# Linear attention with top-1 expert routing: scores by halves of 32 keys, masks of 512 columns, and denominators, logits and ranks in weight sets of 128 columns

## The chip, the cores and the metric

The kernel runs on one core of a Trainium2 chip. The metric is the device time of one execution in microseconds; lower is better. Before the change three runs gave 335.36, 336.8 and 338.79 us, median 336.8 us.

## The reference

One transformer block over x of shape (2, 2048, 128), all in fp32: layer norm and modulation, causal linear attention with 16 heads of 8, a projection, a second norm and modulation, a gate that gives each token one of 8 experts, and that expert's two layers.

```python
q, k, v = jnp.split(h @ w_attn, 3, axis=-1)     # each split into 16 heads of 8
q = elu(q) + 1.0;  k = elu(k) + 1.0
# for every token t, running over all earlier tokens and itself:
#   S += k_t (x) v_t ;  z += k_t ;  y_t = (q_t S) / (q_t . z + 1e-6)
x = x + ga * (y @ w_proj)
h = layernorm(x) * (1 + cb) + sb
logits = h @ Wg + bg;  expert = argmax(logits)
x = x + gb * (gelu(h @ W1[expert]) @ W2[expert])
```

## The kernel before

The 4096 tokens are 32 tiles of 128. A group is four tiles, two consecutive ones (s = 0, 1) of each of the two sequences (b = 0, 1); there are eight groups. Attention inside a tile goes by chunks of L = 64 tokens: what earlier chunks give comes through a running state (`core_across`, L1192 updates it, L1200 multiplies q with it), what the chunk itself gives comes from scores of its 64 keys against its 64 queries, masked so that no query sees a later key.

A unit u = 2s + half is one chunk of both sequences. Per tile, `core_scores` (L1176) makes the scores of four "quads" q of four heads each. `k_q` holds the keys with all rows but the quad's zero; `q_m` holds the queries four times, each time with all heads but one of each quad zero. One matmul has 64 keys of a chunk as weights and 2 x 64 query columns as moving data and writes 64 rows by 128 columns; its two halves (`half`, a pair of heads each) go to rows 0 to 63 and 64 to 127 of a PSUM bank. Two chunks (n) fill 256 columns. Quads alternate between two banks, S0 and S1. On VectorE `core_probs` (L750) multiplies each quad's 256 columns with the mask `causal` into `probs`; `core_within` (L1211) multiplies these with `v_m`, in four column tiles of 32. The work of a tile is issued as FIRST (quads 0, 1) and LAST (quads 2, 3). TensorE waits before each quad until the quad two before it has been masked (`probs_ready`), VectorE before each mask for its scores (`score_mm`).

The step of group g also makes the next group's q, k and v (`front_x` L1123 turns normalised tiles, ScalarE's `front_ht` L486 evacuates them, `front_qkv` L1129, L1131 and, for v, L1135), turns k (`front_kt` L1144, used as k by rows of tokens in `core_across`), makes the denominators' dot products (`front_den` L1154) and turns their reciprocals (`front_inv` L1162). It projects (`core_proj` L1225, evacuated by VectorE's `core_x1` L781). And it routes the group before it: `route_turn` L1234, `route_logits` L1242, `route_rank` L1252 on TensorE; `route_modulate` (L806, L808), `z_and_argmax` and `rden_and_slots` (ending in `slot_i`, L875) on VectorE. With `slot_i` GpSimd scatters the group's rows, tile by tile, to HBM (L411). `core_proj` waits for the slots as well, since it writes the bank that logits and ranks are read from.

`front_den`, `route_logits` and `route_rank` write four column tiles of 32 tokens each, with sets of 32 weight columns; v and turned k use sets of 64.

The order is written out by hand in one function `step` for each engine; all engines run in order and meet at semaphores. After the eight groups the expert stage takes 39 tiles of 128 sorted rows through both layers (L1314, L1321, L1330).

## Time and profile before

| | |
|---|---|
| median of three runs | 336.8 us |
| the profiled execution's own time | 336.95 us |
| its span | 335.2 us |
| PE (TensorE matmul) busy | 266.8 us, 80% |
| DVE (VectorE) busy | 219.9 us, 66% |
| ACT (ScalarE) busy | 158.0 us, 47% |
| POOL (GpSimd) busy | 151.8 us, 45% |
| L1176, scores | 1024 passes, 72.3 us busy, idle 9.1 before them |
| L750, masks | 128 of 420 ns, 51.5 us busy, idle 25.9 before them |

An fp32 matmul shows as two passes, each with its own weight load (PEld), so 512 matmuls are 1024 passes. PE's busy time counts overlapping passes once, and the end of a matmul is modelled. A row of a timeline is a run of instructions of one line: its start, how long until the last one's end, and in brackets the idle time before it with what ended it.

### The profile page before, as it was taken

Reading aid. Unit: us, or ns where it says so; the run is one execution under the profiler, and the core shown is the slowest. Engines: PE = TensorE matmul, PEld = TensorE weight load, DVE = VectorE, ACT = ScalarE, POOL = GpSimd, SP = SyncE. Lnnn points to the kernel's source line nnn. Section 1 sums busy time; section 2 is a strip of 40 time slices with the busy share of each in tenths; the row PEclk is TensorE's granted clock in tenths of the full one; section 3 lists DMA queues with packets and bytes.
Section 4 is the critical chain, followed back from the end, with each engine's and each line's share of the span. In section 5 each row is a group of like instructions: output and inputs, shape, how many; then the busy total and the mean of one; then the engine's idle time right before and its main releaser. Section 6 shows DMA issues by size and latency. Waiting matters only on the chain.

```text
span 335.2 us, 13040 instructions
## 1 busy us (share of the span) xinstructions
PE 266.8 (80%) x5095; PEld 221.5 (66%) x5095; DVE 219.9 (66%) x780; ACT 158.0 (47%) x317; POOL 151.8 (45%) x173
## 2 busy tenths in 40 slices
PE   0564898988798798699699879775949689999990
PEld 0333777676476576567557657664849689999990
DVE  4985539688579478568568768768665645455540
ACT  3059595534345146146065264004525347777740
POOL 8939600352560570471453355330354734455552
PEclk9957899999799899989979999979978959999996
DMA  7990000000100200200200110111673634444410
GB/s 212 336 304 4 0 5 4 3 5 28 72 4 5 98 2 4 98 2 4 91 9 4 57 44 4 55 47 48 182 209 111 231 107 128 128 125 143 132 41 0
DMA packets 17461, 25.85 MB, mean 77 GB/s; under 512 B 2747, under 2 KB 13117, under 8 KB 17410
## 3 DMA queue, kind: packets, MB, share of 16 engines
q1 hardware_dynamic: 13616, 16.12, 16.9%
q0 software_dynamic: 3360, 8.73, 7.3%
q8 instruction: 38, 0.62, 0.8%
q10 hardware_dynamic: 434, 0.27, 0.4%
q14 instruction: 13, 0.11, 0.1%
HBM read 14.78 MB, written 10.78 MB: 76 GB/s over the span
## 4 chain that ended last, share of the span: by engine, by line
PE 52%; DVE 24%; issue 11%; another core or an unknown queue 4%; ACT 4%; DMA 1%; POOL 1%; SPq 1%; POOLq 0%; DVEq 0%; ACTq 0%
PE bank L1176 11%; PE bank L1321 11%; PE bank L1330 10%; DVE probs L750 5%; PE bank L1129 4%; DVE z_t L815 3%; PE bank L1211 2%; DVE row_buf L808 2%; PE bank L1225 2%; DVE row_buf L806 2%; PE bank L1131 2%; DVE mean L660 2%; PE bank L1162 2%; PE bank L1314 1%
## 5 line engine op out<-in xcount | busy, mean ns | idle before, releaser
L1176 PE MATMUL bank<-q_m,k_q 128*64 128x128 f32 x1024 | 72.3, 285 | 9.1 <-DVE probs L750 5.7
L1176 PEld LDWEIGHTS bank<-q_m,k_q 128*64 128x64 f32 x1024 | 56.6, 140 | 18.8 <-DVE probs L750 9.3
L750 DVE TENSOR_TENSOR probs<-bank,causal 128x256 f32<-128x256 f32 x128 | 51.5, 420 | 25.9 <-PE bank L1176 16.5
L411 POOL DMA_INDIRECT sorted_rows<-row_buf,slot_i x32 | 31.6, 988 | 65.5 <-DVE slot_i L875 57.2
L446 POOL DMA_INDIRECT out_dram<-q_m,slot_token x39 | 38.9, 997 | 38.5 <-DVE q_m L1038 25.8
L1321 PE MATMUL bank<-q_m,k_q 128*128 128x128 f32 x312 | 44.0, 287 | 7.4 <-issue 7.4
L1321 PEld LDWEIGHTS bank<-q_m,k_q 128*128 128x128 f32 x312 | 40.4, 203 | 7.9 <-issue 7.9
L1330 PE MATMUL bank<-k_q,v_m 128*128 128x128 f32 x312 | 43.0, 283 | 1.1 <-issue 1.1
L1330 PEld LDWEIGHTS bank<-k_q,v_m 128*128 128x128 f32 x312 | 39.8, 200 | 1.5 <-issue 1.3
L1211 PE MATMUL bank<-probs,v_m 128*32 128x64 f32 x1024 | 21.9, 225 | 16.7 <-DVE probs L750 16.3
L391 POOL TENSOR_TENSOR guess<-var,minus_half 128x4 f32<-128x4 f32 x8 | 8.3, 1039 | 54.2 <-DVE var L663 54.2
L1211 PEld LDWEIGHTS bank<-probs,v_m 128*32 128x32 f32 x1024 | 17.0, 111 | 20.5 <-issue 20.5
L1021 DVE COPY k_q<-w_all 128x512 f32 x39 | 16.9, 436 | 20.6 <-PE bank L1330 17.4
L423 POOL TENSOR_TENSOR k_q<-k_t,quad_rows 128x512 f32<-128x512 f32 x24 | 27.4, 1173 | 2.3 <-DVE k_t L732 2.3
L603 ACT ACTIVATE v_m<-bank 128x512 f32<-128x512 f32 x39 | 23.2, 594 | 9.8 <-PE bank L1321 7.7
L592 ACT ACTIVATE k_q<-w_all 128x512 f32 x39 | 24.4, 630 | 4.1 <-issue 3.6
L545 ACT ACTIVATE h_t<-bank 128x512 f32<-128x512 f32 x8 | 4.8, 598 | 43.4 <-PE bank L1234 43.2
L598 ACT ACTIVATE q_m<-bank 128x128 f32<-128x128 f32 x39 | 10.8, 277 | 23.7 <-PE bank L1314 11.0
L505 ACT ACTIVATE q_m<-q_t,quad_head 128x512 f32<-128x512 f32 x32 | 20.4, 710 | 0.0
L486 ACT ACTIVATE h_t<-bank,sa_col,ca_col 128x256 f32<-128x256 f32 x16 | 8.2, 560 | 25.5 <-PE bank L1123 21.7
L541 ACT ACTIVATE rden<-bank 128x512 f32<-128x512 f32 x8 | 4.8, 597 | 29.9 <-PE bank L1162 29.8
L1135 PEld LDWEIGHTS bank<-wqkv,h_t 128*64 128x64 f32 x256 | 9.0, 151 | 8.6 <-issue 8.6
(208 smaller groups left out, 493.4 us busy)
## 6 DMA issues: line engine op xcount, KB each, us to landing
v_m<-sorted_rows SPq DMA_DIRECT2D x23, 196.0 KB, 2.3
x_all<-in_L_attn_x_dram SPq DMA_DIRECT2D x16, 128.0 KB, 4.2
w_all<-in_L_ffn_W_dram SPq DMA_DIRECT2D x1, 2048.0 KB, 8.7
probs<-sorted_rows SPq DMA_DIRECT2D x10, 196.0 KB, 2.2
sorted_rows<-zeros SPq DMA_DIRECT2D x8, 196.0 KB
q_m<-sorted_rows SPq DMA_DIRECT2D x6, 196.0 KB, 2.6
out_dram<-q_m,slot_token POOLq DMA_INDIRECT x39
sorted_rows<-row_buf,slot_i POOLq DMA_INDIRECT x32
```

Of the source, the lines that this page charges most:

```text
L411: pool.indirect_dma_start(sorted_rows, bass.IndirectOffsetOnAxis(ap=slot_i[par][:, t:t + 1], axis=0), row_buf[par][:, t, :], None).then_in ...
L423: last = nc.gpsimd.tensor_tensor(k_q[par][:, q, :], k_t[par][:], quad_rows[:, q:q + 1].broadcast_to([P, GT * P]), ALU.mult)
L446: pool.indirect_dma_start(out_rows, bass.IndirectOffsetOnAxis(ap=slot_token[ring][:], axis=0), y_row[ring], None, bounds_check=B * T - 1, ...
L505: last = nc.scalar.activation(q_m[par][:, a, :], q_t[par][:], ACT.Copy, scale=quad_head[:, a:a + 1])
L592: nc.scalar.activation(w1_cur[wbuf], w1_all[:, bass.ds((code >> (3 * j)) & (E - 1), 1)].rearrange("p o h -> p (o h)"), ACT.Copy).then_inc( ...
L603: nc.scalar.activation(gelu[par], up_bank[par][:].rearrange("p (k c) -> p k c", k=HC), ACT.Gelu_apprx_tanh).then_inc(gelu_ready, 1)
L750: V.tensor_tensor(probs[:, s, b, q, :], score_bank[q % 2][:, 0:QUADS * L], causal[:].rearrange("p a t -> p (a t)"), ALU.mult).then_inc(pro ...
L1021: V.tensor_copy(w2_cur[wbuf], w2_all[:, bass.ds((code >> (3 * j)) & (E - 1), 1)].rearrange("p o k c -> p (o k) c")).then_inc(w2c_ready, 1)
L1176: last = mm(score_bank[q % 2][L * half:L * half + L, 2 * L * n:2 * L * n + 2 * L], k_q[par][:, q, tok:tok + L], q_m[par][:, 2 * half:2 * h ...
L1211: last = mm(y_bank[half][32 * q:32 * q + 32, b * L:b * L + L], v_m[par][:, 2 * (2 * b + s) + half, a, 32 * q:32 * q + 32], probs[:, s, b, ...
L1321: last = mm(up_bank[par][:, j * P:(j + 1) * P], w1_cur[wbuf][:, j * P:(j + 1) * P], h_col[par], start=True, stop=True)
L1330: last = mm(down_bank[wbuf][:, 0:C], gelu[par][:, j, :], w2_cur[wbuf][:, j, :], start=(j == 0), stop=(j == HC - 1))
```

## The change

The sum of key columns of a chunk is cut in two: scores are made for 32 keys at a time. The weight set has 32 columns, the output 32 rows. Keys 0 to 31 meet all 64 queries (128 moving columns), keys 32 to 63 only queries 32 to 63 (64 moving columns); the quarter that the mask zeroes anyway isn't computed. In the second chunk of each tile the two halves of the keys swap places on the partitions, so that each column tile gets one long and one short matmul of each quad. The rows of v and of turned k must follow, so for odd chunks these are made in two matmuls of 32 columns each (`token_rows`); the mask has the same order on its partitions, made by four selects instead of two.

One bank now holds two quads (512 columns). `core_probs` masks both at once, and TensorE waits once for both. `front_den`, `route_logits` and `route_rank` use sets of 128 weight columns over the full width. The counts of `score_mm` and `probs_ready` are halved where they are waited for.

```diff
--- before.py
+++ after.py
@@ -29,7 +29,7 @@
 NT = B * T // P
 GT = 4
 HEAD, TAIL = slice(0, 2 * GT), slice(2 * GT, NT)
-FIRST, LAST = (0, 1), (2, 3)
+FIRST, LAST = 0, 1
 G = NT // GT
 L = 64
 HC = HID // P
...
@@ -326,9 +326,15 @@
                                     pattern=[[HD, HEADS], [0, HD]], channel_multiplier=-1).then_inc(masks, 1)
             chain.link(nc.gpsimd.memset(causal[:], 1.0))
             for half in range(2):
-                rows = slice(L * half, L * half + L)
-                nc.gpsimd.affine_select(out=causal[rows], in_=causal[rows], compare_op=ALU.is_ge, fill=0.0, base=0,
-                                        pattern=[[0, QUADS], [1, L]], channel_multiplier=-1).then_inc(masks, 1)
+                for part in range(2):
+                    at = L * half + 32 * part
+                    rows = slice(at, at + 32)
+                    last = nc.gpsimd.affine_select(out=causal[rows], in_=causal[rows], compare_op=ALU.is_ge, fill=0.0,
+                                                   base=-32 * part, pattern=[[64 * part - 32, 2], [0, 2], [1, L]],
+                                                   channel_multiplier=-1)
+                    if part == 0:
+                        chain.link(last)
+                last.then_inc(masks, 1)
                 pool.wait_ge(masks, 2 + half)
             for n in range(2):
                 nc.gpsimd.memset(v_m[n][:], 0.0).then_inc(masks, 1)
...
@@ -743,12 +749,13 @@
                 V.tensor_tensor(qz[:], z_t[0][:], q_t[0][:], ALU.mult).then_inc(qz_ready, 1)
                 rden_and_slots(0, 0, 0, chain, True, False)
 
-            def core_probs(g, s, b, quads=range(QUADS)):
+            def core_probs(g, s, b, part):
                 wait_ge(dve, y_mm, 4 * g + 2 * s - 1)
-                for q in quads:
-                    dve.wait_ge(score_mm, 16 * g + 8 * s + 4 * b + q + 1)
-                    V.tensor_tensor(probs[:, s, b, q, :], score_bank[q % 2][:, 0:QUADS * L],
-                                    causal[:].rearrange("p a t -> p (a t)"), ALU.mult).then_inc(probs_ready, 1)
+                dve.wait_ge(score_mm, 8 * g + 4 * s + 2 * b + part + 1)
+                V.tensor_tensor(probs[:, s, b, 2 * part:2 * part + 2, :],
+                                score_bank[part][:].rearrange("p (q t) -> p q t", q=2),
+                                causal[:].rearrange("p n a t -> p (n a t)").unsqueeze(1).broadcast_to(
+                                    [P, 2, QUADS * L]), ALU.mult).then_inc(probs_ready, 1)
 
             def core_state(g, u):
 
...
@@ -1123,6 +1131,13 @@
                     last = nc.tensor.transpose(F0[:, t * P:(t + 1) * P], xhat[:, t, :], ident[:])
                 last.then_inc(xt_mm, 1)
 
+            def token_rows(n, half):
+
+                if n % 2 == 0:
+                    return [(slice(L * half, L * half + L), slice(n * L, n * L + L))]
+                return [(slice(L * half + 32 - 32 * part, L * half + 64 - 32 * part),
+                         slice(n * L + 32 * part, n * L + 32 * part + 32)) for part in range(2)]
+
             def front_qkv(f):
                 pe.wait_ge(ht_ready, f + 1)
                 pe.wait_ge(kn_ready, f)
@@ -1132,8 +1147,8 @@
                 wv = wqkv[:, 2 * C:3 * C].rearrange("p (q h r) -> p q h r", q=QUADS, h=2)
                 for n in range(CHUNKS):
                     for half in range(2):
-                        last = mm(F0[L * half:L * half + L, n * L:(n + 1) * L], h_t[:, n * L:(n + 1) * L],
-                                  wv[:, :, half, :], start=True, stop=True)
+                        for rows, at in token_rows(n, half):
+                            last = mm(F0[rows, n * L:(n + 1) * L], h_t[:, at], wv[:, :, half, :], start=True, stop=True)
                 last.then_inc(v_mm, 1)
 
             def front_kt(f, par):
@@ -1141,18 +1156,17 @@
                 eye = ident[:].rearrange("p (q h r) -> p q h r", q=QUADS, h=2)
                 for n in range(CHUNKS):
                     for half in range(2):
-                        last = mm(F1[L * half:L * half + L, n * L:(n + 1) * L], k_t[par][:, n * L:(n + 1) * L],
-                                  eye[:, :, half, :], start=True, stop=True)
+                        for rows, at in token_rows(n, half):
+                            last = mm(F1[rows, n * L:(n + 1) * L], k_t[par][:, at], eye[:, :, half, :],
+                                      start=True, stop=True)
                 last.then_inc(kt_mm, 1)
 
             def front_den(f):
 
                 pe.wait_ge(qz_ready, f + 1)
                 for t in range(GT):
-                    for j in range(4):
-                        rows = slice(32 * j, 32 * j + 32)
-                        last = mm(F2[rows, HEADS * t:HEADS * t + HEADS], qz[:, t * P + 32 * j:t * P + 32 * j + 32],
-                                  block[:].rearrange("p (h j) -> p h j", j=HD)[:, :, 0], start=True, stop=True)
+                    last = mm(F2[:, HEADS * t:HEADS * t + HEADS], qz[:, t * P:(t + 1) * P],
+                              block[:].rearrange("p (h j) -> p h j", j=HD)[:, :, 0], start=True, stop=True)
                 last.then_inc(den_mm, 1)
 
             def front_inv(f):
@@ -1162,21 +1176,28 @@
                     last = nc.tensor.transpose(F2[:, t * P:(t + 1) * P], qz[:, t * P:(t + 1) * P], ident[:])
                 last.then_inc(inv_mm, 1)
 
-            def core_scores(g, par, s, b, quads=range(QUADS)):
+            def core_scores(g, par, s, b, part):
+
+
                 t = 2 * b + s
                 if s == 0 and b == 0:
-                    pe.wait_ge(qm_ready, g + 1)
-                    pe.wait_ge(kq_ready, 2 * g + 2 if 3 in quads else 2 * g + 1)
-                for q in quads:
-
-                    pe.wait_ge(probs_ready, 16 * g + 8 * s + 4 * b + q + 1)
+                    if part == 0:
+                        pe.wait_ge(qm_ready, g + 1)
+                    pe.wait_ge(kq_ready, 2 * g + part + 1)
+                pe.wait_ge(probs_ready, 8 * g + 4 * s + 2 * b + part + 1)
+                for q in range(2 * part, 2 * part + 2):
                     for n in range(2):
                         tok = t * P + n * L
-                        for half in range(2):
-                            last = mm(score_bank[q % 2][L * half:L * half + L, 2 * L * n:2 * L * n + 2 * L],
-                                      k_q[par][:, q, tok:tok + L], q_m[par][:, 2 * half:2 * half + 2, tok:tok + L],
-                                      start=True, stop=True)
-                    last.then_inc(score_mm, 1)
+                        out_of = score_bank[part][:, 256 * (q % 2) + 128 * n:256 * (q % 2) + 128 * n + 128].rearrange(
+                            "p (a t) -> p a t", a=2)
+                        for keys in (1 - n, n):
+                            for half in range(2):
+                                at = L * half + 32 * (keys ^ n)
+                                last = mm(out_of[at:at + 32, :, 32 * keys:L],
+                                          k_q[par][:, q, tok + 32 * keys:tok + 32 * keys + 32],
+                                          q_m[par][:, 2 * half:2 * half + 2, tok + 32 * keys:tok + L],
+                                          start=True, stop=True)
+                last.then_inc(score_mm, 1)
 
             def core_across(g, par, u):
 
@@ -1202,7 +1223,7 @@
 
             def core_within(g, par, u):
                 s, half = u // 2, u % 2
-                masked = 2 + 16 * g + 8 * s + 8
+                masked = 2 + 8 * g + 4 * s + 4
                 pe.wait_ge(masks, 5)
                 pe.wait_ge(probs_ready, masked)
                 for b in range(B):
@@ -1237,20 +1258,15 @@
             def route_logits(r):
                 pe.wait_ge(h2t_ready, r + 1)
                 for t in range(GT):
-                    for j in range(4):
-                        rows = slice(32 * j, 32 * j + 32)
-                        last = mm(LOGIT[rows, t * E:(t + 1) * E], h2_t[:, t * P + 32 * j:t * P + 32 * j + 32], wg_sb[:],
-                                  start=True, stop=True)
+                    last = mm(LOGIT[:, t * E:(t + 1) * E], h2_t[:, t * P:(t + 1) * P], wg_sb[:],
+                              start=True, stop=True)
                 last.then_inc(logit_mm, 1)
 
             def route_rank(r):
                 pe.wait_ge(onehot_ready, r + 1)
                 hot = onehot[:].rearrange("p n e -> p (n e)")
-                for out_of, table in ((RANK, upper), (TOTAL, ones)):
-                    for j in range(4):
-                        rows = slice(32 * j, 32 * j + 32)
-                        last = mm(out_of[rows], table[:, rows], hot, start=True, stop=True)
-                last.then_inc(rank_mm, 1)
+                mm(RANK, upper[:], hot, start=True, stop=True)
+                mm(TOTAL, ones[:], hot, start=True, stop=True).then_inc(rank_mm, 1)
 
             def step(g, par, front=True, route=True):
                 f, fpar = g + 1, 1 - par
...
```

The places on TensorE that the prediction speaks of, in the middle of a step. First the end of one: projection, the scores of the group's second tile, quads 2 and 3, then transposes and q, k and v of the next group. Names are the tiles, "64x128" is the output (rows = weight columns, then moving columns). Before:

```order
L1225 MATMUL bank0<-wproj_b,y_n 128x128 x3
L1176 MATMUL bank3<-q_m1,k_q1 64x128 [waits probs_ready]
L1176 MATMUL bank3<-q_m1,k_q1 64x128 x3
L1176 MATMUL bank4<-q_m1,k_q1 64x128 [waits probs_ready]
L1176 MATMUL bank4<-q_m1,k_q1 64x128 x3
L1123 MATMUL bank0<-ident,xhat 128x128 [waits x1_ready,v_ready,xhat_ready]
L1123 MATMUL bank0<-ident,xhat 128x128 x3
L1211 MATMUL bank6<-probs,v_m1 32x64 [waits probs_ready,masks]
L1211 MATMUL bank6<-probs,v_m1 32x64 x15
L1129 MATMUL bank1<-h_t,wqkv 128x512 [waits kn_ready,ht_ready]
L1131 MATMUL bank2<-h_t,wqkv 128x512 [waits rden_ready]
L1135 MATMUL bank0<-wqkv,h_t 64x64 x16
```

Now (lines are those of the changed kernel; "2x32" are the 64 short moving columns):

```order
L1246 MATMUL bank0<-wproj_b,y_n 128x128 x3
L1196 MATMUL bank4<-q_m1,k_q1 32x2x32 [waits probs_ready]
L1196 MATMUL bank4<-q_m1,k_q1 32x2x32
L1196 MATMUL bank4<-q_m1,k_q1 32x128 x4
L1196 MATMUL bank4<-q_m1,k_q1 32x2x32 x4
L1196 MATMUL bank4<-q_m1,k_q1 32x128 x4
L1196 MATMUL bank4<-q_m1,k_q1 32x2x32 x2
L1131 MATMUL bank0<-ident,xhat 128x128 [waits x1_ready,v_ready,xhat_ready]
L1131 MATMUL bank0<-ident,xhat 128x128 x3
L1232 MATMUL bank6<-probs,v_m1 32x64 [waits probs_ready,masks]
...
L1151 MATMUL bank0<-wqkv,h_t 64x64 x2
L1151 MATMUL bank0<-wqkv,h_t 32x64 x4
```

The scores of two quads are 16 matmuls instead of 8, in one bank and behind one wait. The last two rows, for v, come four times in turn, so the width of the weight set changes seven times within the line; turned k does the same.

On VectorE, behind the slots, until the masks that let this group's `core_within` begin. Before:

```order
L875 CAST slot_i0<-slot_f 128x4 [waits dve_chain]
...
L750 TENSOR_TENSOR probs<-bank3,causal 128x256 [waits score_mm]
...
L750 TENSOR_TENSOR probs<-bank4,causal 128x256 [waits score_mm]
L768 TENSOR_TENSOR y_n<-bank7,rden1 128x2x64 [waits y_mm]
...
L756 TENSOR_TENSOR state<-bank5,block_b 128x64 [waits kv_mm]
...
L781 TENSOR_TENSOR row_buf1<-x_all,bank0 128x4x128
```

Now:

```order
L755 TENSOR_TENSOR probs<-bank4,causal 128x512 [waits score_mm]
L775 TENSOR_TENSOR y_n<-bank7,rden1 128x2x64 [waits y_mm]
...
L763 TENSOR_TENSOR state<-bank5,block_b 128x64 [waits kv_mm]
...
L755 TENSOR_TENSOR probs<-bank3,causal 128x512 [waits score_mm]
...
L788 TENSOR_TENSOR row_buf1<-x_all,bank0 128x4x128
```

The order of the steps is the same. The two masks behind `slot_i` were of both banks and are now one of bank4 alone; bank3 was masked ahead of the slots.

## Rows read from the trace of the kernel before

**Rows 1.** The page: the chain that ended last, shares of the span by engine

```profile
PE 52%; DVE 24%; issue 11%; another core or an unknown queue 4%; ACT 4%; DMA 1%; POOL 1%; SPq 1%; POOLq 0%; DVEq 0%; ACTq 0%
```

**Rows 2.** Timeline of PE, one step: start us, us until the last end, operation

```profile
115.27 2.08 PE L1129 MATMUL bank<-h_t,wqkv 128*128 128x512 f32 x2
...
120.20 2.28 PE L1176 MATMUL bank<-q_m,k_q 128*64 128x128 f32 x32
122.41 0.65 PE L1211 MATMUL bank<-probs,v_m 128*32 128x64 f32 x32
122.99 1.15 PE L1144 MATMUL bank<-ident,k_t 128*64 128x64 f32 x32
...
125.86 0.66 PE L1234 MATMUL bank<-ident,row_buf 128*128 128x128 f32 x4
126.44 1.09 PE L1176 MATMUL bank<-q_m,k_q 128*64 128x128 f32 x16
...
134.57 1.09 PE L1176 MATMUL bank<-q_m,k_q 128*64 128x128 f32 x16 [0.85 <-DVE probs L750]
...
136.08 1.06 PE L1225 MATMUL bank<-wproj_b,y_n 128*128 128x128 f32 x8
...
138.65 0.63 PE L1123 MATMUL bank<-ident,xhat 128*128 128x128 f32 x4 [0.48 <-DVE row_buf L781]
...
141.78 2.02 PE L1129 MATMUL bank<-h_t,wqkv 128*128 128x512 f32 x2
```

**Rows 3.** Timeline of DVE in the same step

```profile
123.13 0.29 DVE L768 TENSOR_TENSOR y_n<-bank,rden 128x128 f32<-128x128 f32 x1 [0.18 <-PE bank L1211]
...
124.39 1.41 DVE L808 TENSOR_TENSOR row_buf<-row_buf,mod_bc 128x512 f32<-128x512 f32 x1
...
127.93 0.21 DVE L756 TENSOR_TENSOR state<-bank,block_b 128x64 f32<-128x64 f32 x1
...
133.99 0.17 DVE L875 CAST slot_i<-slot_f 128x4 int32<-128x4 f32 x1
...
137.81 0.69 DVE L781 TENSOR_TENSOR row_buf<-x_all,bank 128x512 f32<-128x512 f32 x1 [1.60 <-PE bank L1225]
138.46 0.42 DVE L750 TENSOR_TENSOR probs<-bank,causal 128x256 f32<-128x256 f32 x1
140.63 0.42 DVE L750 TENSOR_TENSOR probs<-bank,causal 128x256 f32<-128x256 f32 x1 [1.75 <-remote]
```

**Rows 4.** Timelines of ACT and POOL at the end of that step

```profile
140.69 1.02 ACT L486 ACTIVATE h_t<-bank,sa_col,ca_col 128x256 f32<-128x256 f32 x2 [3.81 <-PE bank L1123]
...
134.95 1.06 POOL L411 DMA_INDIRECT sorted_rows<-row_buf,slot_i  x1 [9.69 <-DVE slot_i L875]
...
138.85 0.96 POOL L411 DMA_INDIRECT sorted_rows<-row_buf,slot_i  x1 [0.30 <-issue]
```

**Rows 5.** Timelines of PE and ACT at the end of the first step

```profile
58.74 1.06 PE L1225 MATMUL bank<-wproj_b,y_n 128*128 128x128 f32 x8
...
60.75 0.66 PE L1123 MATMUL bank<-ident,xhat 128*128 128x128 f32 x4
...
62.52 1.13 PE L1129 MATMUL bank<-h_t,wqkv 128*128 128x512 f32 x2 [0.43 <-ACT h_t L486]
...
61.45 1.02 ACT L486 ACTIVATE h_t<-bank,sa_col,ca_col 128x256 f32<-128x256 f32 x2 [1.91 <-PE bank L1123]
```

**Rows 6.** Stretches from L1129 to the scores, three steps; behind POOL the granted clock

```profile
62.50:66.10 3.60, 3.58 (x68) 2.17 (x68) 2.00 (x10) 2.25 (x5) 2.10 (x2) 1.00 0.01 2
...
168.60:174.00 5.40, 5.40 (x80) 2.90 (x72) 3.19 (x16) 3.06 (x6) 3.12 (x3) 0.68 0.01 3
195.00:199.00 4.00, 4.00 (x97) 2.48 (x88) 2.72 (x16) 2.70 (x6) 1.73 (x2) 1.00 0.02 6
```

**Rows 7.** Passes of two lines, by source: ns min/median/max, first and last start

```profile
L1176 PE MATMUL bank<-q_m,k_q x128: 272/273/324, 120.2 to 137.9; 128*64 128x128 f32 x128
...
L1211 PE MATMUL bank<-probs,v_m x32: 219/219/243, 122.4 to 122.8; 128*32 128x64 f32 x32
```

12 lines of the change are left out of this document (7 added, 5 removed).

## The prediction

> **What bounds the kernel now.** I read the page first, then steps by window, then one step row by row. The page's chain that ended last [rows 1] is 52% PE and 24% DVE, so neither alone sets the pace. Groups 1 to 6 are pipelined in the attention stage, about 36 to 241 us, where one step (one group of four tiles) takes some 26.5 us: L1129 starts at 115.27 and again at 141.78 [rows 2]. I split this step at the end of `slot_i`, 133.99 + 0.17 = 134.16 [rows 3].
>
> First half, 115.27 to 134.16, 18.9 us: PE and DVE hand work to each other. PE runs q, k, v, then scores; the masks go in turns with them; DVE modulates rows (L806 and L808, until 124.39 + 1.41 = 125.80); PE turns them at 125.86 (L1234); two more masks; then DVE's argmax and slots.
>
> Second half, 134.16 to 141.78, 7.6 us: PE waits for masks (0.85 before the scores at 134.57), projects at 136.08, and turns the next tiles at 138.65 [rows 2]. These four transposes end at 139.28, but ACT's h_t, which waits for nothing else, starts at 140.69; and DVE masks one half of a pair at 138.46 and the other at 140.63, though the scores of both stand before the transposes on PE [rows 2 to 4]. In the first step, with no rows to scatter, ACT started 0.04 after the transposes ended (61.41 to 61.45) [rows 5]. So PE's news arrives late in the scatter steps. The four scatters of POOL run in just that time, 134.95 to 139.81 [rows 4]; what in them holds it the trace doesn't say. From L1225 to L1129 it is 3.78 us in the first step and 5.70 here: **1.9 us a step are this delay**. Behind it comes a lower clock: from L1129 to the scores it is 3.60 at clock 1.00 (62.5 to 66.1), 4.9 here and 5.4 at 0.68 in the step at 168.6 [rows 2, 6].
>
> **The price of a matmul.** Column tiles run side by side: 32 passes of L1211 (four tiles of 32) last 0.65 us, 32 of L1144 (two of 64) 1.15. I call passes that start together a level. A block is its levels plus the last pass's own time [rows 2, 7]: 128 moving columns cost (1.09 - 0.27)/7 = 0.117 a level, 64 cost (0.65 - 0.22)/7 = 0.061, full width (1.06 - 0.27)/7 = 0.113. Changing from one tile width to another: the last L1176 pass before 122.41 starts at 120.20 + 2.28 - 0.27 = 122.21, so 0.08 is lost; from L1211 to L1144 0.09 (122.84 to 122.99 against 0.061). The first level is also 0.02 to 0.05 longer than the later ones (243 against 219 ns, 324 against 273). I take 0.13 a change.
>
> **The change, part by part.**
> - *Scores.* A part (two q) had 8 levels of 128, 1.09 us. Now each column tile has 4 passes of 128 and 4 of 64: 4 x 0.117 + 4 x 0.061 - 0.061 + 0.22 = 0.87. That is 0.22 saved, 8 times a step. Above, if passes of unequal length don't pack, it stays 1.09 or more.
> - *Masks.* Two of 256 columns take 2 x 0.42 = 0.84. For one of 512 out of a bank the nearest row is L781's 0.69 [rows 3]. 0.15 saved, 8 times a step, but the first mask starts only when both q are there: from the start of a part to its last mask was 126.44 to 127.93, 1.49; now 0.88 + 0.69 = 1.57.
> - *v and k_t.* The moved columns stay, but chunks alternate between sets of 64 and of 32: 7 changes of width in each, 0.9 us for v and 0.9 for k_t. The rows show a change only where the line changes too, so the lower bound is 0; I take 0.9, since those changes cost the same in both directions. The Trainium skill (TensorEngine Tiling (Array Packing), Key Properties) says that changing the tiling mode drains TensorE and changing the tile alone doesn't. By that rule 0.9 holds within a line too, and without it the sum would be rival 3's; no row here shows a change within a line.
> - *Denominators, logits, ranks.* 8, 8 and 4 levels of four tiles become as many passes over the full width. The old levels have 8 to 32 moving columns, so at most 0.061 each, some 0.45, 0.45 and 0.25. A new pass lies between that and L1225's 0.113: up to 0.9, 0.9 and 0.45. I take the upper value, the only one with sets of 128.
> - POOL's causal mask: two more selects at its very start, on half the rows each, among memsets that nobody has waited for when PE starts scores. I take nothing; were it uncovered, under 1 us.
> - Fewer waits: a part now waits for the other mask of its own bank, so scores at 134.57 need not wait 0.85.
>
> **The sum for one step, first half.** v delays the scores by 0.90. Four q then run in 1.40 instead of 2.21, but DVE's y_n comes 2.3 after their start (0.88, two masks of 0.69) instead of 2.93 (120.20 to 123.13): h2 is at +0.90 - 0.63 = +0.27. PE gets to L1234 at +0.90 (v) - 0.81 (four q) + 0.90 (k_t) - 0.22 (part) = +0.77, and L1234 stands at h2's heels now, so +0.75 counts. Next part +0.08. Logits: PE is free 0.66 + 0.1 after that part's start, 8 passes of 0.113 and their way out (0.27) end at 1.95; mask and state end at 1.57 + 0.13 = 1.70: +0.25. Ranks the same way +0.1. First half: **+1.2 us**.
>
> Second half. y_n of the fourth unit follows slots and one mask: L1225 at slots + 1.05 instead of + 1.92, because PE's scores are already done. Its end + 0.1, L781 (0.69), and transposes end at slots + 3.7 instead of + 5.1. How late is the news? What ended by 134.16 + 3.0 (L1225) reached DVE 0.6 late (136.08 + 1.06 = 137.14 to L781 at 137.81, less some 0.1 that every wait costs), the second half of the pair 2.4 late. Ending earlier, the transposes should be 0.7 late: h_t 4.4 to 5.4, L1129 at slots + 5.5 instead of + 7.6: **-2.1 us**. Bounds: 0, if nothing gets through before the last scatter, and -2.8 with no delay.
>
> Clock. PE's gap before L1129 is shorter. Four such stretches (88, 115, 142, 169 us) ran low and took 1.3 to 1.8 us more than 3.6, some 6 in all; the step at 195 kept 1.00 behind the same gap [rows 2, 6]. Between 0 and 6 us come back; I take half, 3.
>
> Six steps have scatters behind them: 6 x (1.2 - 2.1) = -5.4; clock -3.0. The first step has no such delay and PE is its path: +0.9 + 0.9 for v and k_t, +0.45 for denominators, -0.22 for some seven parts, +0.7. Before it stand four q on the path (-0.4, two parts) and denominators (+0.45), +0.1. The last step has no v or k_t, and three parts on the path, -0.6. The expert stage keeps its instructions. Sum -5.4 - 3.0 + 0.7 + 0.1 - 0.6 = -8.2. The profiled execution took 336.95 (span 335.2), 0.15 over the median of 336.8. Forecast 328.8, say **329 us**.
>
> **Rivals.**
> 1. *PE's news stays late until the scatters end, the clock too.* Then nothing comes off the second half and the price of narrower sets stands in the first: 6 x 1.2 + 0.7 + 0.1 - 0.6 = +7.4: **344**, slower. For it: the second half of the pair and the transposes both came through at once, 140.6 and 140.7, 0.8 after POOL's last scatter. Against: L1225's and the pair's first half came earlier. It decides if the news of L1123 is more than 2 us late. Chance 0.22.
> 2. *Unequal passes don't pack.* The scores stay at 1.09 a part: 0.22 on some four parts of a step, 7 steps: 6 us less gain, **335**. If a tile with a short pass must wait for the long passes beside it, every level costs 0.117 again. L1211's rows speak for packing, but all of its passes have one length; the issue order, short tiles first, speaks for it too. Chance 0.15. The Trainium skill (TensorE: Matmul & The Clock Gate, The mechanism) has matmuls start and end in program order; read strictly, that is this rival's 335.
> 3. *Changes of width inside a line cost nothing.* Then h2 is what counts in the first half, at -0.63, and it ends at -0.2 instead of +1.2: 7 x 1.4 more, **319**. Chance 0.15.
> 4. *The gain stays small:* half of the 2.1 and no clock: 6 x 0.15 + 0.2 = +1.1, **338**, no change. Chance 0.13.
> The forecast has 0.35.
>
> Range 317 to 344: rival 3 inside, rival 1 at the edge, and the forecast's own bounds (322 with all of the clock and 0.6 more a step, 336 with none and 0.7 less) inside. A difference under 1% (333.4 to 340.2) can't be told from no change. Faster by over 1%: 0.30 of the forecast, 0.15 of rival 3, 0.05 of rival 2, 0.03 of rival 4: 0.53. Slower: rival 1 and some of rival 4: 0.23. Within: the rest, 0.24.
>
> **What would show it.** A part's block of scores at 0.87 (right) or 1.09 (rival 2). v and k_t blocks of about 2.0 instead of 1.15 at full clock (wrong if under 1.3). No wait of PE for a mask before the scores of the next group's second tile; L1225 1.1 after slot_i. ACT's h_t within 1 us of the transposes' end, and L1129 5.5 after slot_i, not 7.6. Clock 1.00 after it in at least three of six steps. Steps of 24.5 to 26 us. The forecast is wrong if h_t still starts 6.5 after slot_i, or if DVE waits over 0.5 for logits.

## The result and the profile after

The changed kernel takes 348.17 us (median of four runs, 347.52 to 350.54), the kernel before 336.08 in the same comparison: 1.032 times as long (95% interval 1.026 to 1.038). Forecast were 329 us, range 317 to 344. It is slower, by the mechanism of rival 1, and 4 us beyond that rival's price.

Three words are used throughout. A *report* (or news) is what tells a waiting engine that PE has ended a piece of work. It is *late* by the time from that end, as the profile models it, to the start of the engine that waits, where that engine stood idle for most of this time. A *hold* is a stretch in which reports come late together.

The page, chain that ended last (answers to [rows 1]), then its lines for the masks and for instruction fetches:

```profile
PE 68%; DVE 11%; another core or an unknown queue 8%; issue 6%; ACT 2%; DMA 1%; POOL 1%; SPq 1%; POOLq 0%; DVEq 0%
...
L755 DVE TENSOR_TENSOR probs<-bank,causal 128x512 f32<-128x512 f32 x64 | 43.9, 690 | 46.9 <-remote 24.9
...
q8 instruction: 45, 0.74, 0.9%
```

The "unknown" share doubled, and of the masks' waits 24.9 us end by nothing that the profile can name (`remote`).

PE, end of one step (answers to [rows 2]); `slot_i` ended here at 103.92 + 0.17 = 104.09:

```profile
104.51 0.66 PE L1176 MATMUL bank<-ident,qz 128*128 128x128 f32 x4
105.05 1.13 PE L1246 MATMUL bank<-wproj_b,y_n 128*128 128x128 f32 x8
106.11 0.87 PE L1196 MATMUL bank<-q_m,k_q 128*32 128x64 f32 x32
107.17 0.63 PE L1131 MATMUL bank<-ident,xhat 128*128 128x128 f32 x4 [0.19 <-DVE row_buf L788]
111.57 1.08 PE L1232 MATMUL bank<-probs,v_m 128*32 128x64 f32 x32 [3.77 <-DVE probs L755]
112.58 1.22 PE L1144 MATMUL bank<-h_t,wqkv 128*128 128x512 f32 x1
```

DVE, ACT and POOL in the same place (answer to [rows 3, 4]):

```profile
106.33 0.69 DVE L788 TENSOR_TENSOR row_buf<-x_all,bank 128x512 f32<-128x512 f32 x1 [0.42 <-PE bank L1246]
110.73 0.69 DVE L755 TENSOR_TENSOR probs<-bank,causal 128x512 f32<-128x512 f32 x1 [3.71 <-remote]
```

```profile
110.79 1.02 ACT L492 ACTIVATE h_t<-bank,sa_col,ca_col 128x256 f32<-128x256 f32 x2 [4.99 <-remote]
```

```profile
104.88 1.06 POOL L417 DMA_INDIRECT sorted_rows<-row_buf,slot_i  x1 [10.35 <-DVE slot_i L882]
...
108.78 0.96 POOL L417 DMA_INDIRECT sorted_rows<-row_buf,slot_i  x1 [0.31 <-issue]
```

Up to the transposes all is as forecast: L1246 starts 0.96 behind the slots (forecast 1.05), the transposes end at 107.80, 3.7 behind them (3.7). Then nothing moves. Scores that ended at 106.98 are masked at 110.73, transposes that ended at 107.80 are picked up at 110.79: 3.0 to 3.8 us late, both at once, 1.0 after POOL's last scatter ended (109.74). In the kernel before the same news was 1.4 to 2.5 late and came 0.8 after the last scatter. From h_t to the q product it is 1.8 instead of 1.1: the held mask is one of 0.69 instead of 0.42, and L1232 behind it takes 1.08 instead of 0.65, at the low clock of the window at 111.0 below.

In two of the five steps it is worse. PE there, where `slot_i` ended at 133.18 and the scatters ran from 133.97 to 138.83:

```profile
135.62 1.06 PE L1246 MATMUL bank<-wproj_b,y_n 128*128 128x128 f32 x8
136.61 0.63 PE L1196 MATMUL bank<-q_m,k_q 128*32 128x64 f32 x8
137.56 0.43 PE L1196 MATMUL bank<-q_m,k_q 128*32 128x128 f32 x6 [0.32 <-issue]
138.33 0.31 PE L1196 MATMUL bank<-q_m,k_q 128*32 128x64 f32 x4 [0.35 <-issue]
139.06 0.22 PE L1196 MATMUL bank<-q_m,k_q 128*32 128x64 f32 x1 [0.41 <-issue]
139.79 0.54 PE L1196 MATMUL bank<-q_m,k_q 128*32 128x64 f32 x13 [0.52 <-issue]
141.28 0.78 PE L1131 MATMUL bank<-ident,xhat 128*128 128x128 f32 x4 [0.95 <-DVE row_buf L788]
...
143.17 2.04 PE L1144 MATMUL bank<-h_t,wqkv 128*128 128x512 f32 x2
```

DVE and ACT there:

```profile
139.78 0.69 DVE L755 TENSOR_TENSOR probs<-bank,causal 128x512 f32<-128x512 f32 x1 [5.45 <-remote]
```

```profile
139.84 0.60 ACT L547 ACTIVATE rden<-bank 128x512 f32<-128x512 f32 x1 [8.79 <-remote]
```

Here the scores ahead of the projection ended at 135.20, 2.0 behind the slots (in the step above 0.5), and their news came at 139.78, 4.6 late. DVE works in order and reads the projection, which ended at 136.68, only behind that mask (L788 at 140.46), so the transposes could only follow. Whether the projection's own news was late as well doesn't show. And PE starts its 32 passes of scores a few at a time, every 0.73 to 0.95 us, where the block above took 0.87 in all.

Windows, behind POOL the granted clock (answer to [rows 6]): the first step, a stretch before `slot_i`, two stretches behind the hold.

```profile
57.40:60.80 3.40, 3.03 (x48) 1.55 (x48) 2.25 (x16) 2.06 (x4) 1.05 (x1) 1.00 0.02 5
...
111.00:117.80 6.80, 6.23 (x60) 3.04 (x60) 3.67 (x19) 3.27 (x6) 3.13 (x3) 0.50 0.01 2
131.40:134.90 3.50, 3.50 (x117) 3.27 (x109) 2.70 (x11) 0.00 (x0) 0.93 (x1) 0.51 0.02 5
...
169.00:175.80 6.80, 5.97 (x56) 2.89 (x58) 3.82 (x18) 3.35 (x6) 3.13 (x3) 0.50 0.02 6
```

0.50 is the lower level, 1.2 of 2.4 GHz. Before the change such a stretch behind a hold was 3.4 us long; now it is 6.8 in two of the five steps, and there is a new one ahead of the slots (131.4, and again at 189.5). It stands in just the two steps in which the scores and the projection are late behind the slots: L1246 starts at slots + 2.4 there instead of + 1.0.

Mean of five steps, split as in the prediction (q product to end of `slot_i`, and from there to the next q product), for all kernels of this study. "Stalls": the distance from the start of one pass to the start of the next, where it is over 0.45 us, summed inside blocks of one PE line, q, k and v products aside, 57 to 200 us. Whole times (medians of all runs) are compared only along a row, with the kernel before on the same chip; those in brackets are single runs that leave scatters out. Ratios compare only the fast runs of both kernels, and the traces of e1, e4, e9 and e15 are of runs over 1.5% above the fastest of their kernel, so small differences in their steps carry little.

| kernel | first half | second half | step | stalls | whole | kernel before |
|---|---|---|---|---|---|---|
| before | 18.86 | 7.70 | 26.56 | 1.0 | | 336.08 |
| changed | 19.64 | 8.96 | 28.60 | 5.1 | 348.17 | 336.08 |
| e1 v, k_t in sets of 32 | 20.13 | 9.17 | 29.30 | 17.9 | 348.04 | 337.15 |
| e2 narrow denominators etc. | 19.21 | 8.41 | 27.62 | 14.6 | 341.72 | 337.15 |
| e3 both | 19.20 | 8.59 | 27.80 | 26.1 | 343.41 | 337.15 |
| e4 before, wide denominators etc. | 19.09 | 7.99 | 27.08 | 0.5 | 341.98 | 337.15 |
| e5 changed, no scatters | 18.44 | 5.09 | 23.53 | 0.5 | (313.49) | |
| e6 before, no scatters | 18.14 | 5.71 | 23.85 | 1.0 | (315.20) | |
| e7 before, late scatters | 20.81 | 5.71 | 26.52 | 11.2 | 342.25 | 337.47 |
| e8 e3, late scatters | 21.56 | 5.21 | 26.77 | 25.9 | 340.79 | 337.47 |
| e9 before, spread | 20.72 | 5.71 | 26.43 | 0.5 | 332.31 | 336.25 |
| e10 e3, spread | 20.44 | 5.20 | 25.64 | 13.1 | 331.08 | 336.25 |
| e11 e2, no scatters | 18.20 | 5.61 | 23.81 | 9.6 | (317.11) | |
| e12 e1, no scatters | 19.05 | 5.09 | 24.14 | 17.0 | (320.68) | |
| e13 before, paced | 18.14 | 5.71 | 23.85 | 1.0 | 313.62 | 308.79 |
| e14 changed, paced | 18.51 | 5.59 | 24.10 | 0.5 | 312.09 | 308.79 |
| e15 e2, paced | 18.30 | 6.37 | 24.67 | 13.0 | 311.72 | 308.79 |
| e16 e3, paced | 18.22 | 5.81 | 24.03 | 24.0 | 314.87 | 308.79 |
| e17 changed, paced, again | 18.73 | 5.42 | 24.15 | 0.6 | 323.41 | 339.17 |
| e18 changed, again | 19.64 | 8.82 | 28.47 | 2.5 | 349.26 | 339.17 |

Of the span's 346.4 - 335.2 = 11.2 us, five steps give 5 x 2.04 = 10.2; from the last q product to the end it is 145.0 instead of 139.9, +5.1, all of it before the slots of the seventh group (44.5 instead of 39.2), so still in the attention stage; and the first full step starts 4.1 earlier (58.4 instead of 62.5).

These 4.1 us have nothing to do with scores. The very first q product starts at 16.00 instead of 20.73. VectorE in the first norm, and GpSimd's fills beside it, before and now:

```profile
9.35 5.30 DVE L660 TENSOR_SCALAR mean<-mean 128x8 f32<-128x8 f32 x1
...
12.73 1.83 POOL L338 MEMSET k_n<- 128x1024 f32 x2
```

```profile
9.63 0.64 DVE L666 TENSOR_SCALAR mean<-mean 128x8 f32<-128x8 f32 x1
...
6.70 3.55 POOL L340 MEMSET v_m<- 128x2048 f32 x2
```

The small VectorE instruction ends within 0.1 us of the end of one of these fills: before at 14.65 (fills of k_n until 14.56), now at 10.27 (fills of v_m until 10.25). The two more selects for the causal mask put the fills 1.0 us later. In all 14 traces with the changed selects the instruction took 0.56 to 1.19 us; with those of the kernel before it took 5.2 to 5.5 in four (the kernel before, e4, e9, e13) and 1.6 in two (e6, e7). So the gain goes with the changed selects, but no run changes them alone, and only traced runs show it. By an estimate from these traces, the change would stand some 16 us above the kernel before without this gain.

### The profile page after: what moved, and what is told of

Its sections match the earlier page's. It is cut to its first block, busy times and chain, and to the rows that moved or that the text cites. A ratio compares the mean times of both kernels' runs of the same rounds, so it can differ in the third digit from the quotient of the medians.

```text
span 346.4 us, 14531 instructions
## 1 busy us (share of the span) xinstructions
PE 287.7 (83%) x5895; PEld 239.3 (69%) x5895; DVE 207.6 (60%) x716; ACT 158.6 (46%) x317; POOL 151.1 (44%) x175
## 4 chain that ended last, share of the span: by engine, by line
PE 68%; DVE 11%; another core or an unknown queue 8%; issue 6%; ACT 2%; DMA 1%; POOL 1%; SPq 1%; POOLq 0%; DVEq 0%
PE bank L1338 10%; PE bank L1196 10%; PE bank L1347 10%; PE bank L1151 5%; PE bank L1160 5%; PE bank L1144 4%; PE bank L1232 4%; DVE z_t L822 3%; PE bank L1146 3%; PE bank L1168 3%; PE bank L1261 3%; PE bank L1221 2%; PE bank L1246 2%; DVE probs L755 2%
## 5 line engine op out<-in xcount | busy, mean ns | idle before, releaser
L755 DVE TENSOR_TENSOR probs<-bank,causal 128x512 f32<-128x512 f32 x64 | 43.9, 690 | 46.9 <-remote 24.9
L1196 PE MATMUL bank<-q_m,k_q 128*32 128x128 f32 (+1 forms) x2048 | 60.4, 262 | 4.7 <-issue 3.1
L1196 PEld LDWEIGHTS bank<-q_m,k_q 128*32 128x32 f32 x2048 | 49.9, 117 | 12.7 <-issue 7.1
L1232 PE MATMUL bank<-probs,v_m 128*32 128x64 f32 x1024 | 25.6, 251 | 17.9 <-DVE probs L755 17.6
L1232 PEld LDWEIGHTS bank<-probs,v_m 128*32 128x32 f32 x1024 | 20.4, 128 | 20.6 <-issue 20.0
L1029 DVE COPY k_q<-w_all 128x512 f32 x39 | 16.9, 435 | 20.6 <-PE bank L1347 17.0
L429 POOL TENSOR_TENSOR k_q<-k_t,quad_rows 128x512 f32<-128x512 f32 x24 | 26.5, 1137 | 4.7 <-DVE k_t L738 4.7
L604 ACT ACTIVATE q_m<-bank 128x128 f32<-128x128 f32 x39 | 10.7, 277 | 25.9 <-PE bank L1331 13.5
L1151 PEld LDWEIGHTS bank<-wqkv,h_t 128*32 128x32 f32 (+1 forms) x384 | 12.5, 127 | 13.6 <-issue 9.3
```

The lines of the kernel that those rows point to most:

```text
L429: last = nc.gpsimd.tensor_tensor(k_q[par][:, q, :], k_t[par][:], quad_rows[:, q:q + 1].broadcast_to([P, GT * P]), ALU.mult)
L755: V.tensor_tensor(probs[:, s, b, 2 * part:2 * part + 2, :], score_bank[part][:].rearrange("p (q t) -> p q t", q=2), causal[:].rearrange("p ...
L1151: last = mm(F0[rows, n * L:(n + 1) * L], h_t[:, at], wv[:, :, half, :], start=True, stop=True)
L1196: last = mm(out_of[at:at + 32, :, 32 * keys:L], k_q[par][:, q, tok + 32 * keys:tok + 32 * keys + 32], q_m[par][:, 2 * half:2 * half + 2, t ...
L1232: last = mm(y_bank[half][32 * q:32 * q + 32, b * L:b * L + L], v_m[par][:, 2 * (2 * b + s) + half, a, 32 * q:32 * q + 32], probs[:, s, b, ...
```

## The experiments

**e1 to e4: which part of the change.** e1, uniform sets in v and turned k:

```diff
 def token_rows(n, half):
-    if n % 2 == 0:
-        return [(slice(L * half, L * half + L), slice(n * L, n * L + L))]
-    return [(slice(L * half + 32 - 32 * part, ...
+    swap = n % 2
+    return [(slice(L * half + 32 * (part ^ swap), ...
...
```

> The changed kernel, but v and the transposed k write all 8 chunks in weight sets of 32 columns (64 products instead of 48 a front, both blocks together), so that no block changes its set's width inside. Theory W (the width changes inside these two blocks are what the change lost): each block falls from 2.13 us to 1.2, 1.9 us a step over 7 steps and the first front, so about 13 us less than the change's 348: 334 to 337, and the first half of a step comes back from 20.6 to about 18.9 us. Theory R (TensorE's reports come late after the scatters, whatever the widths, and the extra instructions make it worse): the blocks get shorter, but the last reports of a step still come 4 us late at the scatters' end, and with 16 more products a front the time stays at 343 to 349. Theory N (a change of width costs the same wherever it is and only the number of instructions counts): blocks at 2.1 or more, 348 or more.

Measured: the blocks fall from 2.13 to 1.10, but the whole stays: 348.04.

```profile
121.57 1.10 PE L1150 MATMUL bank<-wqkv,h_t 128*32 128x64 f32 x64
124.86 0.73 PE L1159 MATMUL bank<-ident,k_t 128*32 128x64 f32 x34
126.27 0.59 PE L1159 MATMUL bank<-ident,k_t 128*32 128x64 f32 x27 [0.68 <-issue]
```

So 7 changes of width cost 1.03, 0.15 each, also inside a line. But new stalls appear, 17.9 us in all, as in the third row. Theory W fails for the whole, and the time is in theory R's range.

e2, with `front_den`, `route_logits` and `route_rank` as in the kernel before:

```diff
 for t in range(GT):
-    last = mm(F2[:, HEADS * t:HEADS * t + HEADS], qz[:, t * P:(t + 1) * P], ...
+    for j in range(4):
...
+        last = mm(F2[rows, HEADS * t:HEADS * t + HEADS], qz[:, t * P + 32 * j:...
```

> The changed kernel, but denominators, logits and ranks again in four sets of 32 columns each, as before the change. Theory W (widths alone): full-width passes cost 1.06 us for a block of four products against about 0.15 to 0.3, 0.9 + 0.9 + 0.45 us a step: with all of it on the path 348 - 16 = 332, with half hidden 340. Theory R (late reports set the second half of a step): the pattern of late reports stays, gain only the part of the denominators in front of the hold: 342 to 346. Theory C (the new half-clock stretch at 131 to 135 us comes from the full-width passes, in which few columns move): that stretch goes, and the time falls by 1.5 to 3 us more than the blocks' own shortening.

341.72 (1.020 times before, 1.009 to 1.032): 6.4 us back, the larger of the two parts. The half-clock stretch at 131 is gone, as theory C had it, and with it the second halves of 10 us (they are 8.2 to 8.6). Late reports stay, up to 2.6 us. Some come through between the scatters here: the mask at 135.86 and ACT's rden at 136.57, 2.3 and 2.5 late, before the last scatter (136.98 to 137.94) had started.

e3 puts both edits together.

> Both edits: the changed scores and masks with every other product of the front in sets of 32 columns, no 64- or 128-column set beside them but in q, k, transposes and projections. Theory W: the sum of the two gains, 348 - 13 - 8 to 16 = 319 to 329, below the kernel before (336). Theory R: 338 to 345, since the late reports after the scatters stay.

343.41, in theory R's range: no sum of gains; stalls 26.1 us.

e4, the kernel before with the wide products alone:

> The kernel before, with only the denominators, logits and ranks in sets of 128 columns (the third part of the change alone). Theory W: +0.9 +0.9 +0.45 us a step at most, on the path for a half to all of it: 336 + 7 to 16 = 343 to 352. Theory R: the wide products fall where TensorE waits for news anyway: 336 to 340. If 12 fewer products a step shorten the delay of the reports, 333 to 336.

341.98, ratio 1.012 (0.991 to 1.034), unclear, and between the ranges of W and R; its steps are 0.5 us longer, partly in each half. Together: no width explains a second half of 8 to 9 us.

**e5, e6: without the scatters.**

```diff
 def route_scatter(r, par):
+    if r < G - 2:
+        return
...
```

Waits for these scatters are lowered, and SyncE fetches one fixed tile for the experts, so the output isn't the reference's: the steps can be compared with those above, the whole times only between such runs.

> The changed kernel without the 24 scatters of groups 0 to 5 (the experts then read rows of zeros and write nothing from them, so only the time of the attention steps is compared; the output is not the reference's). Theory R (TensorE's completion reports are held back while the scatters of a step run, and the release sets the next step's start): no report is over 0.2 us late, the two patterns of steps vanish, slot_i to the next q falls from 8.5 and 10.0 us to 4.5 to 6 (the prediction's 5.5), and the period of a step from 28 to 30.6 to 24 to 26 us. Theory Q (TensorE itself is what stalls there, for instance for its instructions, and the scatters only stand beside it): reports stay 3 to 4.5 us late, periods 27 to 30.

> The kernel before, without the same 24 scatters (the same part of the computation left out). Theory R: reports on time, slot_i to the next q from 7.65 to 5.5 to 6.5 us, a step from 26.7 to 24.5 to 25.5: the prediction's second half would then be true only relative to this kernel: the changed kernel without scatters should be 0 to 1.5 us a step faster or slower than it. Theory Q: unchanged at 26.7.

Theory R holds. In these steps no report is over 0.2 us late, and steps of 23.53 and 23.85 are even under the ranges (24 to 26, 24.5 to 25.5). PE and ACT of e5, `slot_i` at 122.27:

```profile
123.23 1.13 PE L1247 MATMUL bank<-wproj_b,y_n 128*128 128x128 f32 x8
...
125.35 0.63 PE L1132 MATMUL bank<-ident,xhat 128*128 128x128 f32 x4 [0.19 <-DVE row_buf L789]
126.06 0.65 PE L1233 MATMUL bank<-probs,v_m 128*32 128x64 f32 x32
127.09 1.12 PE L1145 MATMUL bank<-h_t,wqkv 128*128 128x512 f32 x2 [0.37 <-ACT h_t L493]
```

```profile
126.01 1.02 ACT L493 ACTIVATE h_t<-bank,sa_col,ca_col 128x256 f32<-128x256 f32 x2 [2.03 <-PE bank L1132]
```

ACT starts 0.03 after the transposes' end, and q at slots + 4.8. The scatters cost the kernel before 26.56 - 23.85 = 2.7 us a step and the changed one 28.60 - 23.53 = 5.1. Without them the change is 0.3 us a step faster. The half-clock stretches behind q are gone in both kernels too; e5 has one left, ahead of the slots of its fourth step, where the second half is 6.11 instead of 4.82 to 4.86.

**e7, e8: the scatters elsewhere.** Behind the next step's k_q products. e8 is the same on e3's kernel; it was expected to have a second half of 5.5 us and 325 to 349 by theory R, 343 by theory Q:

```diff
                 front_kq(r + 2, par)
-                route_scatter(r, par)
+                if r >= 1:
+                    route_scatter(r - 1, 1 - par)
...
```

> The kernel before, with each group's four scatters moved from right behind its slot indices to behind the next step's k_q products on GpSimd (about 16 us later in the program, around the second tile's second block of scores). Theory R: the hold of reports moves there too; at its new place news of scores, logits and states is needed every 1 to 2 us, so the step gets 2 us shorter at the old place and 0 to 4 us longer at the new: 325 to 348, with the late reports all at the new place. Theory Q: nothing late at the new place, and the old place as late as it was: 336.

The second half is 5.71, the first 21.5 in the steps with scatters: the hold moved along, as theory R had it, and the time, 342.25 (1.024, 1.013 to 1.036), is in its range. In e8 the halves are 5.21 and 21.56, the whole 340.79 (1.016, 1.004 to 1.028). PE and DVE in e7, while the second to fourth scatter ran (120.50 to 124.00):

```profile
121.62 0.41 PE L1213 MATMUL bank<-probs,v_m 128*32 128x64 f32 x4 [0.25 <-DVE probs L752]
122.47 0.32 PE L1213 MATMUL bank<-probs,v_m 128*32 128x64 f32 x4 [0.44 <-issue]
123.20 0.32 PE L1213 MATMUL bank<-probs,v_m 128*32 128x64 f32 x5 [0.41 <-issue]
123.93 0.32 PE L1213 MATMUL bank<-probs,v_m 128*32 128x64 f32 x5 [0.41 <-issue]
124.66 0.41 PE L1213 MATMUL bank<-probs,v_m 128*32 128x64 f32 x12 [0.41 <-issue]
```

```profile
124.80 0.19 DVE L825 TENSOR_TENSOR logit<-bank,bg_bc 128x32 f32<-128x32 f32 x1 [3.20 <-remote]
```

This is the mechanism at its plainest: from the second scatter of four on, PE starts four or five passes every 0.73 to 0.85 us, and its news (here of the logits) waits until 0.8 after the last (124.00 to 124.80).

**e9, e10: scatters one at a time**, behind the slots, the guess, the norm and the k_q products.

> The kernel before, with each group's four scatters spread over a step: the first right behind the slot indices, the others behind the next step's guess, its normed rows and its k_q products. Theory S (TensorE is held only where scatters follow each other within 1.3 us, since the first one of a group held nothing in any trace so far; one alone costs nothing): the 2.9 us a step that the scatters cost come back, 336 - 6 x 2.9 + the fifth that moves to the end = about 319 to 323. Theory T (each scatter holds TensorE for about its own 1 us, wherever it is): 3 of 4 still cost, 330 to 335, and the late reports show 0.5 to 1 us at each of the four places. Theory U (the place alone matters, and three places inside the step are worse than the one behind the slots): 337 to 345.

> The changed scores and masks with v and the transposed k in sets of 32 columns, denominators, logits and ranks narrow, and the scatters spread in the same way. Theory S: the run without the spread took 343 with a second half of 8.3 to 9.6 us and late reports of 2.4 to 4.5; with the second half at 4.9 it is 343 - 6 x 3.7 = 318 to 323. Theory T: 330 to 338. Theory U: 338 to 350.

e9: 0.986 (0.980 to 0.993); no report over 0.35 late, as theory S had it, and the second half 5.71, but 332.31 us misses its 319 to 323 (it lies in theory T's range, whose late reports are absent), since the first half is 21.3 to 21.5 in the steps with spread scatters. GpSimd begins the k_q products 0.8 us later behind q (6.4 instead of 5.5), and VectorE's first multiply by the scale, now beside them right behind a scatter, took 3.8 us in each of these steps (1.4 to 1.5 in e6), 2748 ns on average instead of the 958 of the kernel before:

```profile
L814 DVE TENSOR_TENSOR row_buf<-row_buf,mod_bc 128x512 f32<-128x512 f32 x8 | 22.0, 2748 | 1.3 <-POOL row_buf L402 1.3
```

e10: 331.08, 0.985 (0.981 to 0.989), 1.5% below the kernel before and again above theory S (318 to 323). Its latest reports are 1.1 late.

**e11, e12: widths where nothing is held.**

> The changed kernel without the 24 scatters (that part of the computation is left out), and with denominators, logits and ranks narrow again: sizes the full-width passes where nothing is held. The run without scatters took 23.25 us a step, its first half 18.4. Theory W (all of the blocks' own 2.0 us longer is on the path): 21.2 us a step. If half is beside waits for the masks: 22.2. If hidden: 23.2.

> The changed kernel without the 24 scatters (left out as above), and with v and the transposed k all in sets of 32 columns: sizes the changes of width where nothing is held. Theory W: 1.9 us a step less, 21.4 us. If v's end is beside ScalarE's work and only the transposed k counts: 22.3. If the product count sets the time: 23.2 or more.

Neither is shorter than e5 (23.81 and 24.14 against 23.53). The first halves can be (18.1 and, in e12's best step, 17.4 instead of 18.4), but stalls take it back. PE in e11:

```profile
171.18 0.29 PE L1199 MATMUL bank<-q_m,k_q 128*32 128x64 f32 x4
172.51 0.80 PE L1199 MATMUL bank<-q_m,k_q 128*32 128x128 f32 x26 [1.04 <-issue]
```

e11 has 6375 passes and 48 instruction fetches of 16 KB, e5 5895 and 45. The seven stalls over 0.8 us begin 0.8 to 2.0 us after such a fetch starts and end 1.2 to 1.6 after it ends, and so do the twelve of e12 (0.5 to 1.7, and 1.2 to 1.6); I read them as PE running out of instructions. The number of passes alone doesn't order them: e12 has 6151 and 17.0 us of stalls. The Trainium skill (Runtime: NRT & Kernel Launch, Instruction fetch mechanics) calls the cost of such a fetch mostly hidden; in e11 it wasn't, if that reading is right, which no run isolates.

**e13 to e16: paced**, each scatter where GpSimd is idle: behind the slots; when x1 is there; behind the k_q products; when the next logits are there.

```diff
 for t in turns:
+    if t == 1 and len(turns) == 1:
+        pool.wait_ge(x1_ready, r + 3)
+    if t == 3 and len(turns) == 1:
+        pool.wait_ge(logit_mm, r + 2)
     pool.indirect_dma_start(...)
...
-                route_scatter(r, par)
+                if r >= 1:
+                    route_scatter(r - 1, 1 - par, [2])
+                    route_scatter(r - 1, 1 - par, [3])
+                route_scatter(r, par, [0])
+                route_scatter(r, par, [1])
...
```

> The kernel before, its scatters paced: the first behind the slot indices, the second when the sums x1 are there, the third behind the next step's k_q products, the fourth when that step's logits are there, all where GpSimd has nothing else to do. Theory S (only scatters that stand back to back hold TensorE): no report over 0.3 us late, a step of 23.8 to 24.5 us, 336 - 6 x 2.5 = 319 to 323. Theory T (each scatter holds TensorE for its own microsecond): 25.5 to 27 us a step, 328 to 336.

> The changed kernel with the same pacing and nothing else. Theory S: 23.3 to 24.5 us a step as without scatters, 348 - 6 x 4.5 = 319 to 323, level with or up to 3 us below the paced kernel before: the change would then be worth the prediction's sign only where the hold is away. Theory T: late reports of 1 us at each scatter, 333 to 340.

> As the run above, with denominators, logits and ranks narrow. Without scatters this variant's first half was 0.3 us shorter and its second 0.7 longer than the changed kernel's, with more stretches at the half clock: 318 to 326. If the narrow products shorten the path wherever the hold is away: 315 to 318.

> As the run above, with v and the transposed k in sets of 32 columns too. The spread version of it took 331.1. With steps of 25.7 us there and norm and multiply no longer late: 24 us a step, 318 to 324. If the many small products bring the half clock back at the slots (0.903 there): 325 to 330.

The steps are those without scatters: 23.85 and 24.10, inside theory S's ranges. But on this chip the kernel before took 308.79 itself, and the paced kernels 1.02 to 1.03 times that: here pacing the kernel before cost 2% (313.62, 1.022, 1.009 to 1.035), and the times forecast for all four (318 and more by their first theories) were missed by 3 to 7 us. Two things differ on this chip. From the last `slot_i` to the end, where all kernels run the same expert instructions, it is 68.5 to 69.2 us in the four traces here and 72.6 to 75.7 in all others. And late reports are missing there too: in the stretch from the seventh group's slots on, in which GpSimd scatters the experts' rows (L446) 39 times, the idle time that they give VectorE and ScalarE, counted where it is over 0.3 us, adds up to 7 us here and to 17 to 23 elsewhere. So the hold seems to be much smaller on this chip, also in the kernel before: 336 us with steps of 26.6 can't shrink to 309 by these 7 us alone. That kernel left no trace here, so for it this stays argued. Among the four, no part of the change shows a difference beyond 1%; and e14's first q product starts 4.3 us ahead of e13's (16.4 and 20.7, the fills at the start again), so behind it the changed kernel is the longer one, by 3.9 us of the spans.

**e17, e18: on one more chip**, the paced changed kernel and the changed kernel.

> The changed kernel with paced scatters once more, word for word. Theory H (back-to-back scatters hold TensorE on some chips and not on others): if the kernel before takes 336 here, this one takes 312 to 320, since it has no hold on either kind of chip; if the kernel before takes 309, this one takes 312 again. Theory P (the whole chip was faster by 8% last time, pacing or not): where the kernel before takes 336, this one takes 336 to 342.

> The changed kernel, word for word. Theory H: where the kernel before takes 336, 348 again with reports 3 to 4.5 us late; where it takes 309, no late reports, steps of 23.3 us and 305 to 309, level with it or faster. Theory P: 1.03 times the kernel before on either kind of chip.

The kernel before took 339.17 here. The change: 349.26, 1.032 (1.023 to 1.042), the first result again. The same kernel paced: **323.41, 0.959 (0.950 to 0.967)**, 26 us less, faster than both. Theory H had 312 to 320, 3 us too low: behind the last slots it is 74.6 us here. The kernel before wasn't paced on this chip. PE, POOL and ACT of the paced kernel, `slot_i` at 104.64:

```profile
107.72 0.63 PE L1141 MATMUL bank<-ident,xhat 128*128 128x128 f32 x4 [0.19 <-DVE row_buf L798]
108.44 0.66 PE L1242 MATMUL bank<-probs,v_m 128*32 128x64 f32 x32
109.46 1.12 PE L1154 MATMUL bank<-h_t,wqkv 128*128 128x512 f32 x2 [0.37 <-ACT h_t L502]
```

```profile
105.42 0.96 POOL L421 DMA_INDIRECT sorted_rows<-row_buf,slot_i  x1 [5.20 <-DVE slot_i L892]
108.38 0.96 POOL L421 DMA_INDIRECT sorted_rows<-row_buf,slot_i  x1 [2.00 <-DVE row_buf L798]
...
118.86 1.31 POOL L421 DMA_INDIRECT sorted_rows<-row_buf,slot_i  x1 [0.17 <-issue]
122.83 0.96 POOL L421 DMA_INDIRECT sorted_rows<-row_buf,slot_i  x1 [2.67 <-PE bank L1271]
```

```profile
108.39 1.02 ACT L502 ACTIVATE h_t<-bank,sa_col,ca_col 128x256 f32<-128x256 f32 x2 [2.04 <-PE bank L1141]
```

q stands at slots + 4.8, though a scatter starts beside ACT's h_t. The latest report of a step is 1.1 us late here (0.9 to 1.1 in five steps in a row, of scores that end beside the third scatter); in e14, the same kernel on the other chip, none is over 0.2 late: theory H, shown for the late reports by one trace on either chip.

## Why the prediction was wrong, step by step

- *Scores, masks, widths, wide passes*: right. A part is 0.87 (forecast 0.87), so unequal passes pack and rival 2 is false. A mask is 0.690 (0.69). v and k_t are 2.13 (2.0), 0.15 a change by e1, so rival 3 is false. Denominators and logits are 1.06 a block (0.9). The Trainium skill (TensorE: Matmul & The Clock Gate, The mechanism) has matmuls start and end in program order; read strictly that would have given 1.09 a part, and the measured 0.87 decides against that reading. The rule of the Trainium skill (TensorEngine Tiling (Array Packing), Key Properties) that a change of tiling mode drains TensorE agrees with e1's 0.15.
- *First half, +1.2*: +0.3 without scatters (e5, e6), +0.8 with them. What the scatters add goes with longer half-clock stretches: the first halves are 20.5 and 20.6 in the two steps that begin with 6.8 us of it, and 18.4 to 19.5 in the others. The sign was right, the size too large: the blocks grew as priced, so part of their time ran beside other engines' work.
- *Second half, -2.1*: **the step that failed.** Its instructions moved as worked out, to 0.1 us. But "ending earlier, the transposes should be 0.7 late" took the delay as something that news meets by its distance from the slots, from one row that ended at slots + 3.0 and got through 0.6 late. The transposes were to end at slots + 3.7, nearer to the scores that ended at + 4.0 and came 2.4 late, so even that row didn't bear the 0.7. What the runs show in its place is a hold until 0.8 to 1.0 us after the last scatter; the transposes were 3.0 late instead of 0.7. The release came at slots + 6.7 (before 6.5), the wider mask and the low clock behind it added 0.7, so q stood at slots + 8.5 instead of + 5.5, and at slots + 10.0 where the scores ahead of the projection were caught too. Over the five steps the second half is +1.3 a step instead of -2.1: 17 of the 19 us between forecast and result.
- *Clock, -3*: wrong sign. The stretches come behind the hold, so they didn't go but grew, and e5 and e6 have none there.
- *Before the first step, +0.1*: -4.1, from GpSimd's mask at the start, of which the prediction said "I take nothing" and feared under 1 us of cost. The traces show a gain of 4.7 us up to the first q product, by the place of the fills beside VectorE's small instruction. As far as it is the change's, that part of the result is luck.
- *The frame*: with scatters that hold nothing the changed kernel's second half is 0.6 us shorter than before's, 5.09 to 5.71, and 0.3 is left per step. So even then the change would have been worth about 2 us (313.5 to 315.2 without scatters, one run each, 0.8 of it before the first q product), not 8.
- *Rival 1* had the mechanism and the deciding point (news of the transposes over 2 us late) and 344, but not the sum: it had nothing on the second halves, which grew by 6.3 us over five steps (3.0 of them in the two steps of 10.0), and 6.0 on the first, which grew by 3.9. That it came within 4 us is in part the 4.1 us of the start. I had its best evidence in the prediction, two reports released together 0.8 behind the last scatter, and gave it 0.22.
